# Three engines' orders changed inside the turn, and one joint stretch in place of the last three turns

## The chip, the cores and the metric

The kernel runs on one core of a Trainium2 chip. The metric is the device time of one execution in microseconds; lower is better. The core's engines run side by side, each through its own list of instructions, and wait for each other by semaphores: TensorE (PE, matmuls and transposes), VectorE (DVE), ScalarE (ACT), GpSimd (POOL) and SyncE (SP, which here issues the DMAs).

## What is computed

For 32 sequences of 512 tokens, three stages with residual sums. Cut to what matters:

```python
h = tok(x, mask)                 # running counts of each skill, mapped to 64 features
h = h + attn(layernorm(h))       # a decayed linear-attention recurrence over the batches' positions
h = h + ffn(layernorm(h))        # mixture of 8 experts, the best 2 weighted by softmax

def ffn(x):                      # xn = layernorm(x) * gamma + beta
    logits = xn @ Wr + br;  w = softmax of the top 2, scattered over 8 experts
    for e in range(8):
        h_e = gelu(xn @ W1[e] + b1[e]);  y += (h_e @ W2[e] + b2[e]) * w[:, e]

def attn(v):                     # per step: x_t = (0.97*x + relu(v @ Dx.T)) / sum
    a = rho @ x_t;  y = relu(ln(a) @ Dy.T) * relu(x_t);  out = ln(y @ E.T);  rho = 0.97*rho + outer(ln(v), x_t)
```

## The kernel before, in words

After a preamble (counts, features, factors) the kernel goes through the 32 batches in turns. A batch is 512 tokens (4 chunks of 128). Turn i does four things at once, each for another batch: the attention of batch i (`att`), the residual and the centring of batch r = i - 1 (`res`), the router of batch t = i - 2 (`rt`), and the experts of batch k = i - 3 (`mlp`). Batch i - 4 is finished (`done`), and the inputs of batch i + 1 are made ready (`ahead`). Turns 0 to 3 fill the pipe, turns 4 to 29 are a loop of two turns a round, turns 30 and 31 are written out, and turns 32, 33 and 34 empty the pipe without attention. Each engine has its own `turn` function: its order of calls is the order in which the engine works, and nothing overtakes.

One turn, by what hangs on what:

- TensorE: `scores(i, 0..3)` (L1331) from the scanned inputs `xs` into two PSUM banks; `input_rows` and `state_of` for the carried state (L1342, L1353); `values` (L1366, L1370); `y_core` (L1392); `attn_var`; `update(i + 1, 0)` and `update(i + 1, 1)` (L1320), the pre-activation of the next batch, each into the bank that a gate has read; `z_out` (L1412); `z_rows` (L1421). Between them stand the router's `centred_T` and `logits` (L1431, L1440), eight `hidden(k, e)` (two matmuls each, L1449 and L1450, into two banks in turn), four `expert_out(k, q)` (L1461), `weights_T` (L1469) and `fold` (L1485).
- VectorE: `diagonal(i, 0..3)`, the causal mask on a scores block (L985); `residual(r)` (L1016), which waits for GpSimd's z_scaling; the router in small steps (L1021 to L1063); `weigh(k, q)` (L1072), the expert output times its weights; `gate` (L1001); `scan_input` (L970) and two scans (L979) for the next turn; `finish` (L992).
- ScalarE: `gelu(k, e)` (L605), one for each hidden; copies of PSUM (`centred_T` L598, `weights_T` L616, `z_T` L621, `attn_T` L584); `centred_high(r)` (L593), the f16 high part of the centred input; `z_square` (L628) and `h_square` (L636).
- GpSimd: `z_scale` (L423, L426), `centred` (L431 to L437), `centred_input` (L410), `centred_low(r)` (L447), which waits for `centred_high`, then `mean_back(r)` (L442) and `weighted_input(i + 1)` (L417), then `add_pairs` (L453), which waits for the scans; `add_halves` and `add_experts` (L457, L463).
- SyncE: stores a batch's router weights to DRAM and reads them back broadcast over the partitions (`spread`, two DMAs of 512 KB), loads the scan's factors, stores the output.

Hidden 0..7 use two banks, so `hidden(k, e)` waits for `gelu(k, e - 2)`. `scores(i, 3)` waits for `diagonal(i, 1)`, since both use one bank. `scores(i, 0)` waits for both scans.

Of the kernel before, what the change touches and what calls it, by code (L numbers as in the profile page):

```python
# [24 lines left out]
P = 128  # L25
# [6 lines left out]
E = 8  # L32
# [44 lines left out]
def program(nc, x, r, skill_w, skill_b, att_w, att_b, mast_w, mast_b, proj_w, proj_b, Ea, Dx, Dy, gamma, beta,  # L77
            Wr, br, W1, b1, W2, b2, ident, masks, decays, out):
    with ExitStack() as ctx:
# [116 lines left out]
        last_acc, last_both = relu_b[:, 0, :], relu_b[:, 1, 0:S // 2]  # L196
# [3 lines left out]
        ld_w3 = sem("ld_w3")  # L200
        ld_rows = [sem(f"ld_rows{n}") for n in range(4)]
# [39 lines left out]
        dv_relu, dv_sum = sem("dv_relu"), sem("dv_sum")  # L241
# [24 lines left out]
        def of_half(rows, half):  # L266

            chunks = rows.rearrange("p (c n) -> p c n", c=C)
            return chunks[:, 0:C:C - 1] if half == 0 else chunks[:, 1:C - 1]

# [7 lines left out]
        def _(sp):  # L278
# [47 lines left out]
            def store(b):  # L326
                sp.wait_ge(dv_out, b + 1)
                sp.dma_start(out[bass.ds(b, 1)].rearrange("o (c p) d -> p (o c) d", p=P), o_sb[:]).then_inc(st_out, 16)

            def spread(b, side):  # L330
# [32 lines left out]
        def _(pool):  # L363
# [102 lines left out]
            def turn(i, att, res, rt, mlp, done, ahead, side):  # L466
# [15 lines left out]
                if mlp and (not isinstance(i, int) or i < B + 2):  # L482
# [16 lines left out]
            turn(B, False, True, True, True, True, False, 0)  # L499
            turn(B + 1, False, False, True, True, True, False, 1)  # L500
            turn(B + 2, False, False, False, True, True, False, 0)
# [3 lines left out]
        def _(act):  # L505
# [94 lines left out]
            def gelu(b, e):  # L600
# [4 lines left out]
                act.activation(hid[:, e, :], h_bank[e % 2][:, :], ACT.Gelu, bias=b1T[:, e:e + 1],  # L605
# [34 lines left out]
            def turn(i, att, res, rt, mlp, done, ahead, side):  # L640
                r, t, k = i - 1, i - 2, i - 3
                if rt and not (isinstance(i, int) and i > B):
                    centred_T(t, side)
# [25 lines left out]
                if res:  # L669
                    centred_high(r)  # L670
                if rt:
                    weights_T(t)
                if mlp:
                    gelu(k, 5)
                    gelu(k, 6)
# [16 lines left out]
            turn(B, False, True, True, True, True, False, 0)  # L692
            turn(B + 1, False, False, True, True, True, False, 1)
            turn(B + 2, False, False, False, True, True, False, 0)
# [3 lines left out]
        def _(dve):  # L698
# [377 lines left out]
            def last_sum(q):  # L1076

                dve.wait_ge(dv_tm, NP * (B - 1) + q + 1)
                wait(dve, dv_sum, q - 1)
                dve.tensor_tensor(last_acc, tm[:, 0, :] if q == 1 else last_acc, tm[:, q, :], ALU.add).then_inc(dv_sum, 1)  # L1080

            def last_halves():
                dve.wait_ge(dv_sum, NP - 1)
                dve.tensor_tensor(last_both, last_acc[:, 0:S // 2], last_acc[:, S // 2:S], ALU.add).then_inc(dv_sum, 1)

            def turn(i, att, res, rt, mlp, done, ahead, side):
# [28 lines left out]
                final = isinstance(i, int) and i == B + 2  # L1115
# [9 lines left out]
                if final:  # L1125
                    last_sum(1)
# [8 lines left out]
                if mlp:  # L1135
                    weigh(k, 2, 1 - side)
                    if final:
                        last_sum(2)
                    weigh(k, 3, 1 - side)
                if final:  # L1140
                    last_sum(3)
                    last_halves()
# [13 lines left out]
            turn(B, False, True, True, True, True, False, 0)  # L1156
            turn(B + 1, False, False, True, True, True, False, 1)
            turn(B + 2, False, False, False, True, True, False, 0)
            finish(B - 1)
# [3 lines left out]
        def _(pe):  # L1163
# [260 lines left out]
            def centred_T(b):  # L1424
# [4 lines left out]
                wait(pe, dv_out, b - 2)  # L1429
# [35 lines left out]
            def weights_T(b):  # L1465

                pe.wait_ge(dv_w, b + 1)
                wait(pe, dv_out, b - 2)
                pe.transpose(ly_w, w_flat[:], ident_f[:]).then_inc(pe_wT2, 1)  # L1469

            def fold(b):

                total = both
                if isinstance(b, int) and b == B - 1:
                    pe.wait_ge(dv_sum, NP)
                    total = last_both
                else:
                    pe.wait_ge(po_acc, b + 1)
                if isinstance(b, int):
                    pe.wait_ge(ac_wT, min(b + 3, B))  # L1480
                else:
                    pe.wait_ge(ac_wT, b + 3)
                for c in range(2):
                    y = ly[:, 256:512].rearrange("p (n c d) -> p c n d", n=2, c=2)[:, c]
                    last = pe.transpose(y, total[:, c * P:(c + 1) * P], ident_f[:])  # L1485
                last.then_inc(pe_fold, 1)

            def turn(i, att, res, rt, mlp, done, ahead, side):
                r, t, k = i - 1, i - 2, i - 3
                ending = isinstance(i, int) and i > B  # L1490
                if att:
                    scores(i, 0)
                if rt and not ending:
# [8 lines left out]
                if rt and not ending:  # L1502
# [8 lines left out]
                if mlp:  # L1511
                    hidden(k, 3, 1 - side)
                    if ending:
                        expert_out(k, 0)
                    if not att:
# [110 lines left out]
```

## Time and profile before

| | us |
|---|---|
| median of 3 runs | 698.47 (698.41 to 698.85) |
| profiled execution | 698.65 |
| its span, first to last instruction | 696.9 |
| busy: TensorE, VectorE, ScalarE, GpSimd | 636.0, 552.2, 436.6, 341.8 |
| mean granted TensorE clock | 0.99 of full speed |

Times in the profile are microseconds from the start of the span. A busy share says how full an engine is, not who waits for whom; a group of instructions has a line of the kernel, a count, a time and what released the engine before it. PE stands for matmuls and PEld for the weight loads ahead of them, which overlap matmuls.

### The profile page before, as it was taken

The page shows a single profiled execution, that of the slowest core. Times are in us where ns is not written, and L with a number is a line of the kernel's source. Part 1 is how long each engine was busy: PE and PEld are TensorE (multiplying, and loading weights), DVE is VectorE, ACT ScalarE, POOL GpSimd, SP SyncE. Part 2 cuts the span into 40 slices and gives each one's busy share as a digit, 9 for nine tenths or more (in the row PEclk, how much of TensorE's full clock was granted, in tenths as well). Part 3 has the DMA queues.
Part 4 walks back from the last instruction along what each step waited for, and adds up shares of the span by engine and source line. Part 5 has one row for each costly group of instructions (what it writes and reads, how often), then busy time and mean ns, then how long its engine had stood idle before and what let it go on. Part 6 is the DMA issues. An engine that isn't in the chain of part 4 may idle for free.

```text
span 696.9 us, 19160 instructions
## 1 busy us (share of the span) xinstructions
PE 636.0 (91%) x5027; PEld 428.5 (61%) x5064; DVE 552.2 (79%) x1956; ACT 436.6 (63%) x1385; POOL 341.8 (49%) x440
## 2 busy tenths in 40 slices
PE   1582997989999999999999999999999999999986
PEld 0472774456666666666666666666666666667542
DVE  4998888976688888888788888887888888887574
ACT  6980997024566666666666666666666666666663
POOL 2000001933465665566666665566656655666552
PEclk9999998899999999999999999999999999999999
DMA  6200000011434444444445444444444444454444
GB/s 214 98 0 1 1 0 1 25 40 35 94 92 102 99 99 99 112 111 109 111 110 117 117 101 99 99 99 99 99 99 99 99 99 114 106 111 100 94 80 84
DMA packets 61295, 60.41 MB, mean 87 GB/s; under 512 B 21796, under 2 KB 56724, under 8 KB 60756
## 3 DMA queue, kind: packets, MB, share of 16 engines
q1 hardware_dynamic: 58836, 59.34, 35.7%
q10 hardware_dynamic: 2240, 0.73, 0.5%
q8 instruction: 13, 0.21, 0.1%
q14 instruction: 14, 0.11, 0.0%
q0 software_dynamic: 192, 0.01, 0.0%
HBM read 55.18 MB, written 4.89 MB: 86 GB/s over the span
## 4 chain that ended last, share of the span: by engine, by line
PE 75%; DVE 10%; ACT 8%; issue 5%; ACTq 1%; DMA 1%; SPq 0%; DVEq 0%
PE bank L1461 16%; PE bank L1331 13%; PE bank L1449 7%; PE bank L1450 6%; PE bank L1392 5%; PE bank L1412 4%; PE bank L1353 4%; ACT skill_rows L605 3%; PE bank L1366 3%; PE bank L1237 2%; PE bank L1370 2%; PE bank L1342 2%; PE bank L1188 2%; PE bank L1226 2%; PE bank L1217 2%
## 5 line engine op out<-in xcount | busy, mean ns | idle before, releaser
L605 ACT ACTIVATE skill_rows<-bank,b1T,w_scale 128x512 f32<-128x512 f32 x256 | 195.1, 777 | 60.7 <-PE bank L1450 59.2
L1461 PE MATMUL bank<-skill_rows,w_sb 128*64 128x256 f32 x1024 | 128.6, 383 | 0.0
L453 POOL TENSOR_TENSOR feat_parts<-skill_rows 128x512 f32<-128x512 f32 x62 | 78.9, 1272 | 75.7 <-DVE feat_parts L979 67.8
L1331 PE MATMUL bank<-feat_parts 128*128 128x256 f32 (+1 forms) x512 | 104.4, 337 | 1.4 <-DVE feat_parts L979 0.9
L1461 PEld LDWEIGHTS bank<-skill_rows,w_sb 128*64 128x64 f32 x1024 | 69.1, 137 | 42.5 <-issue 12.9
L1331 PEld LDWEIGHTS bank<-feat_parts 128*128 128x128 f32 x512 | 77.3, 190 | 12.0 <-DVE feat_parts L985 6.5
L1001 DVE SCALAR_TENSOR_TENSOR feat_parts<-bank,feat_parts 128x256 f32<-128x256 f32 x128 | 45.4, 418 | 46.1 <-PE bank L1392 46.1
L979 DVE TENSOR_TENSOR_SCAN feat_parts<-same,feat_parts 128x512 f32<-128x512 f32 x62 | 74.3, 1238 | 0.0
L1072 DVE SCALAR_TENSOR_TENSOR skill_rows<-bank,b2T,feat_parts 128x256 f32<-128x256 f32 x128 | 54.2, 474 | 7.6 <-issue 4.8
L628 ACT ACTIVATE bank<-bank 128x64 f32<-128x64 f32 x128 | 26.7, 221 | 50.9 <-PE bank L1421 50.9
L1072 DVE SCALAR_TENSOR_TENSOR skill_rows<-bank,b2T,skill_rows 128x256 f32<-128x256 f32 x128 | 54.3, 473 | 4.2 <-PE bank L1461 2.9
L568 ACT ACTIVATE feat_parts<-bank 128x128 f32<-128x128 f32 x64 | 17.6, 275 | 61.6 <-DVE feat_parts L985 61.6
L1016 DVE SCALAR_TENSOR_TENSOR h_all<-bank,z_scaling,h_all 128x64 f32 (+1 forms) x128 | 27.5, 278 | 31.6 <-POOL z_scaling L426 31.6
L1449 PE MATMUL bank<-xT_even,w1k 128*128 128x512 f16 x128 | 48.8, 381 | 2.7 <-ACT skill_rows L605 1.8
L1449 PE MATMUL bank<-xT_odd,w1k 128*128 128x512 f16 x128 | 48.8, 381 | 2.3 <-ACT skill_rows L605 1.3
L1450 PE MATMUL bank<-xT_odd,w1k 128*128 128x512 f16 x128 | 48.5, 379 | 0.0
L1450 PE MATMUL bank<-xT_even,w1k 128*128 128x512 f16 x128 | 48.5, 379 | 0.0
L431 POOL TENSOR_TENSOR h_var<-h_sq,eps_sq 128x4 f32<-128x4 f32 x32 | 6.5, 203 | 80.9 <-ACT h_squares L636 80.9
L457 POOL TENSOR_TENSOR feat_parts<-feat_parts 128x512 f32<-128x512 f32 x31 | 39.3, 1269 | 2.4
L970 DVE SCALAR_TENSOR_TENSOR feat_parts<-bank,same 128x512 f32<-128x512 f32 x62 | 39.7, 681 | 0.0
L985 DVE TENSOR_TENSOR feat_parts<-bank,mask_sb 128x128 f32<-128x128 f32 x128 | 35.6, 278 | 4.0 <-PE bank L1331 3.8
L1392 PE MATMUL bank<-aT,dyT 64*128 64x256 f32 x256 | 36.3, 402 | 0.0
(266 smaller groups left out, 1446.1 us busy)
## 6 DMA issues: line engine op xcount, KB each, us to landing
skill_rows<-w_d SPq DMA_DIRECT2D x32, 512.0 KB, 6.5
feat_parts<-w_d SPq DMA_DIRECT2D x32, 512.0 KB, 6.3
same<-factor_d SPq DMA_DIRECT2D x31, 512.0 KB, 5.2
skill_rows<-skill_row_d SPq DMA_DIRECT2D x4, 1024.0 KB, 7.8
out<-o_sb SPq DMA_DIRECT2D x32, 128.0 KB, 4.9
w_sb<-in_L_ffn_W ACTq DMA_DIRECT2D x2, 256.0 KB
w_d<-wT SPq DMA_DIRECT2D x32, 16.0 KB, 1.4
table_k<-table_d SPq DMA_DIRECT2D x9, 2.5 KB
```

Of the source, the lines that this page charges most:

```text
L453: pool.tensor_tensor(half[:, n, :], tm[:, 2 * n, :], tm[:, 2 * n + 1, :], ALU.add).then_inc(po_half, 1)
L457: pool.tensor_tensor(acc.rearrange("p two t -> p (two t)"), half[:, 0, :], half[:, 1, :], ALU.add)\
L605: act.activation(hid[:, e, :], h_bank[e % 2][:, :], ACT.Gelu, bias=b1T[:, e:e + 1], scale=w1_scale[:, e:e + 1]).then_inc(ac_gelu, 1)
L970: dve.scalar_tensor_tensor(relu_b[:, k, :], n_bank[k][:, :], 0.0, factor[:, 1, :], ALU.max, ALU.mult)\
L979: dve.tensor_tensor_scan(xs[:, k, :], factor[:, 0, :], relu_b[:, k, :], 0.0, ALU.mult, ALU.add)\
L1001: dve.scalar_tensor_tensor(of_half(ys[:, k], half), core[:, k], 0.0, of_half(xs[:, k], half), ALU.max, ALU.mult).then_inc(dv_y, 1)
L1072: last = dve.scalar_tensor_tensor(tm[:, q, cols], z_bank[q % 2][:, cols], b2T[:, e:e + 1], wb[side][:, e, :], ALU.add, ALU.mult)
L1331: last = pe.matmul(n_bank[sc % 2][:, 0:SPAN[sc]], xs[:, k, sc * P:(sc + 1) * P], xs[:, k, sc * P:sc * P + SPAN[sc]], start=(k == 0), stop= ...
L1392: last = pe.matmul(n_bank[half][:, k * 2 * P:(k + 1) * 2 * P], dyT[rows, k * P:(k + 1) * P], aT[rows, :], start=True, stop=True)
L1449: pe.matmul(h_bank[e % 2][:, :], w1k[:, 0, e, :], xT[side][:], start=True, stop=False)
L1450: pe.matmul(h_bank[e % 2][:, :], w1k[:, 1, e, :], xT[side][:], start=False, stop=True).then_inc(pe_hid, 1)
L1461: last = pe.matmul(z_bank[q % 2][n * D:(n + 1) * D, at:at + S // 2], w2_sb[:, e, :], hid[:, e, n * (S // 2):(n + 1) * (S // 2)], start=Tru ...
```

## The change

Inside a turn, three orders change. VectorE does `diagonal(i, 1)` before `residual(r)`. ScalarE does `weights_T(t)` and `gelu(k, 5)` before `centred_high(r)`. TensorE does `hidden(k, 6)` between the two `update` calls.

Turn 31 now also holds `centred_T` and `logits` of batch 30, on TensorE and ScalarE. Turns 32 to 34 and the last fold go. In their place each engine gets a `drain()` for batches 29, 30 and 31 together. In it the hiddens use four banks, the expert outputs three banks by a written list, the two GpSimd sums of the last batch are replaced by transposes that accumulate in PSUM (`last_fold`), the last batch's weights are read back in four DMAs with two semaphores, and the last four stores have output tiles of their own. The matmuls that only kept TensorE busy there (`keep_running`) go.

```diff
@@ scalar turn
                 if mlp:
                     gelu(k, 4)
+                if rt:
+                    weights_T(t)
+                if mlp:
+                    gelu(k, 5)
                 if res:
                     centred_high(r)
-                if rt:
-                    weights_T(t)
-                if mlp:
-                    gelu(k, 5)
+                if mlp:
                     gelu(k, 6)
                     gelu(k, 7)
-                if isinstance(i, int) and i == B:
+                if isinstance(i, int) and i == B - 1:
                     centred_T(r, 1 - side)
@@ vector turn
                 if att:
                     diagonal(i, 0)
+                    diagonal(i, 1)
                 if res:
                     residual(r)
-                if att:
-                    diagonal(i, 1)
@@ tensor turn
                 if ahead:
                     update(i + 1, 0)
+                if mlp:
+                    hidden(k, 6, 1 - side)
+                if ahead:
                     update(i + 1, 1)
-                if mlp:
-                    hidden(k, 6, 1 - side)
...
+                if done:
+                    fold(i - 4)
+                if mlp:
                     hidden(k, 7, 1 - side)
-                if isinstance(i, int) and i == B:
+                if before_drain:
                     centred_T(r)
                 if att:
                     z_out(i)
...
@@ sync
+            def spread_last(side):
+                sp.wait_ge(ac_wT, B)
+                sp.dma_start(w_d[side].rearrange("e (c p) -> (e c) p", c=C), wT[:]).then_inc(st_w, 16)
+                sp.wait_ge(st_w, 16 * B)
+                for late, signal in enumerate((ld_wb, ld_wb_late)):
+                    experts = slice(late * NP, (late + 1) * NP)
+                    for n in range(2):
+                        rows = w_d[side:side + 1, experts, n * (S // 2):(n + 1) * (S // 2)]
+                        sp.dma_start(wb[side][n * D:(n + 1) * D, experts], rows.to_broadcast([D, NP, S // 2]))\
+                          .then_inc(signal, 16)
...
-            turn(B, False, True, True, False, 0)
-            turn(B + 1, False, True, True, False, 1)
-            turn(B + 2, False, False, True, False, 0)
-            store(B - 1)
+            spread(B - 2, 0)
+            spread_last(1)
+            for n in range(4):
+                store(B - 4 + n, last_o[n])
@@ gpsimd
+            def drain():
+                z_scale(B - 1)
+                add_pairs(B - 4, 1)
+                centred(B - 1)
+                centred_low(B - 1)
+                add_halves(B - 4)
+                add_experts(B - 4)
+                mean_back(B - 1)
+                for b in (B - 3, B - 2):
+                    add_pairs(b, 0)
+                    add_pairs(b, 1)
+                    add_halves(b)
+                    add_experts(b)
@@ scalar
+            def drain():
+                a, b, c = B - 3, B - 2, B - 1
+                for e in range(3):
+                    gelu(a, e, drain_h)
+                h_square(c)
+                tanh(b)
+                for e in range(3, 6):
+                    gelu(a, e, drain_h)
+                centred_high(c)
+                weights_T(b)
+                for e in range(6, E):
+                    gelu(a, e, drain_h)
+                centred_T(c, 1)
+                for e in range(4):
+                    gelu(b, e, drain_h)
+                tanh(c)
+                for e in range(4, 6):
+                    gelu(b, e, drain_h)
+                weights_T(c)
+                for e in range(6, E):
+                    gelu(b, e, drain_h)
+                for e in range(E):
+                    gelu(c, e, drain_h)
@@ vector
+            def drain():
+                a, b, c = B - 3, B - 2, B - 1
...
+                residual(c)
...
+                drain_weigh(a, 0)
+                drain_weigh(a, 1)
+                drain_weigh(a, 2)
...
+                merge(c, m)
+                drain_weigh(a, 3)
+                drain_finish(B - 4)
+                for q in range(NP):
+                    drain_weigh(b, q)
+                drain_finish(a)
+                for q in range(NP):
+                    drain_weigh(c, q)
+                drain_finish(b)
+                last_finish()
@@ tensor
+            def drain():
+                a, b, c = B - 3, B - 2, B - 1
+                for e in range(6):
+                    drain_hidden(a, e)
+                drain_out(a, 0)
+                drain_hidden(a, 6)
+                drain_out(a, 1)
+                weights_T(b)
+                drain_hidden(a, 7)
+                drain_out(a, 2)
+                drain_hidden(b, 0)
+                centred_T(c)
...
+                drain_out(a, 3)
+                logits(c, 1)
...
+                drain_out(b, 1)
+                weights_T(c)
...
+                drain_fold(B - 4)
+                for e in range(4):
+                    drain_hidden(c, e)
+                drain_out(b, 2)
+                drain_out(b, 3)
+                drain_hidden(c, 4)
+                drain_hidden(c, 5)
+                drain_out(c, 0)
+                drain_hidden(c, 6)
+                drain_hidden(c, 7)
+                drain_fold(a)
+                drain_out(c, 1)
+                for e in range(2):
+                    last_fold(0, e)
+                drain_out(c, 2)
+                for e in range(2):
+                    last_fold(1, e)
+                drain_out(c, 3)
+                drain_fold(b)
+                for q in range(2, NP):
+                    for e in range(2):
+                        last_fold(q, e)
```

`before_drain` is turn 31. In the VectorE stretch `residual(c)` stands inside the router of b, and `merge(c)` ends the whole router of c. `drain_weigh`, `drain_out` and `drain_hidden` do what `weigh`, `expert_out` and `hidden` do, with the banks and waits of the new stretch; `drain_weigh(c, 2)` and `drain_weigh(c, 3)` also wait for the later two of the four DMAs, and `drain_out(b, 3)` waits for `drain_weigh(b, 0)`, whose bank it takes.

## Rows read from the trace of the kernel before

**Rows 1.** Busy time of each engine over the whole execution, from the page.
```profile
PE 636.0 (91%) x5027; PEld 428.5 (61%) x5064; DVE 552.2 (79%) x1956; ACT 436.6 (63%) x1385; POOL 341.8 (49%) x440
```

**Rows 2.** Waits, 411.7 to 641.9: who for whom; us in total, times, longest.
```profile
PEld bank L1449 <- ACT skill_rows L605: 3.8, 13, 0.3
...
PEld bank L1331 <- DVE feat_parts L985: 2.6, 13, 0.2
```

**Rows 3.** Timeline of one turn: start, us, engine, line, operation [idle before <- releaser].
```profile
406.30 0.78 ACT L605 ACTIVATE skill_rows<-bank,b1T,w_scale 128x512 f32<-128x512 f32 x1 [1.80 <-PE bank L1450]
...
406.98 0.40 ACT L593 ACTIVATE x_p<-xc 128x256 f16<-128x256 f32 x1
...
407.28 0.25 ACT L616 ACTIVATE wT<-bank 32x128 f32<-32x128 f32 x1
...
407.44 2.23 ACT L605 ACTIVATE skill_rows<-bank,b1T,w_scale 128x512 f32<-128x512 f32 x3
407.46 0.68 POOL L447 TENSOR_TENSOR x_p<-xc,x_p 128x256 f16<-128x256 f32 x1 [0.97 <-ACT x_p L593]
...
408.25 0.39 PE L1449 MATMUL bank<-xT_odd,w1k 128*128 128x512 f16 x1
...
408.67 0.61 POOL L417 TENSOR_TENSOR same<-h_all,u_scale 128x256 f32 x1
...
409.06 2.41 DVE L979 TENSOR_TENSOR_SCAN feat_parts<-same,feat_parts 128x512 f32<-128x512 f32 x2
...
409.70 1.90 PE L1461 MATMUL bank<-skill_rows,w_sb 128*64 128x256 f32 x16
...
411.80 1.03 PE L1331 MATMUL bank<-feat_parts 128*128 128x256 f32 x4
...
412.67 0.39 PE L1431 MATMUL bank<-ident_h,x_p 128*128 128x128 f16 x4
...
414.21 0.38 PE L1449 MATMUL bank<-xT_even,w1k 128*128 128x512 f16 x1
...
414.74 1.61 PE L1331 MATMUL bank<-feat_parts 128*128 128x256 f32 x8
...
416.19 0.38 PE L1449 MATMUL bank<-xT_even,w1k 128*128 128x512 f16 x1
```

**Rows 4.** Timeline, turn 0 into turn 1: scans, then the scores that wait.
```profile
151.99 2.33 DVE L979 TENSOR_TENSOR_SCAN feat_parts<-same,feat_parts 128x512 f32<-128x512 f32 x2
...
154.37 1.13 PE L1331 MATMUL bank<-feat_parts 128*128 128x256 f32 x4 [0.32 <-DVE feat_parts L979]
```

**Rows 5.** The bias add: all 32 (least/median/most ns), one beside GpSimd's add.
```profile
L1026 DVE TENSOR_TENSOR lg<-lg,br_sb x32: 191/1198/1232, 171.3 to 672.8; 128x32 f32<-128x32 f32 x32
...
201.76 1.27 POOL L457 TENSOR_TENSOR feat_parts<-feat_parts 128x512 f32<-128x512 f32 x1
...
201.88 1.20 DVE L1026 TENSOR_TENSOR lg<-lg,br_sb 128x32 f32<-128x32 f32 x1
```

**Rows 6.** Timeline of the end, from turn 31's first scores on.
```profile
642.09 1.03 PE L1331 MATMUL bank<-feat_parts 128*128 128x256 f32 x4
...
658.20 0.44 PE L1421 MATMUL bank<-ident_f,zT_sb 128*128 128x128 f32 x2
...
661.09 0.86 DVE L1016 SCALAR_TENSOR_TENSOR h_all<-bank,z_scaling,h_all 128x64 f32<-128x64 f32 x4 [1.89 <-POOL z_scaling L426]
...
663.80 0.24 ACT L636 ACTIVATE h_squares<-h_all 128x64 f32<-128x64 f32 x1
...
667.08 0.42 ACT L593 ACTIVATE x_p<-xc 128x256 f16<-128x256 f32 x1 [1.57 <-POOL xc L437]
667.41 0.25 ACT L616 ACTIVATE wT<-bank 32x128 f32<-32x128 f32 x1
...
677.16 1.66 DVE L1072 SCALAR_TENSOR_TENSOR skill_rows<-bank,b2T,skill_rows 128x256 f32<-128x256 f32 x4 [0.23 <-DMA skill_rows<-w_d]
...
694.04 0.42 DVE L992 TENSOR_TENSOR o_sb<-bank,h_all 128x256 f32<-128x256 f32 x1 [0.53 <-PE bank L1485]
```

More of the change, by code:

```diff
@@ L195, in program @@
         both = sb("both", [P, S // 2])
-        last_acc, last_both = relu_b[:, 0, :], relu_b[:, 1, 0:S // 2]
+        last_tm = over(parts_flat, 2 * S, NP, S)
+        last_o = [over(parts_flat, n * C * D, C, D) for n in range(4)]
         o_sb = sb("o_sb", [P, C, D])
@@ L604, in gelu @@
                 wait(act, pe_zz, NP * (b - 1) + e // 2 + 1)
[L605 removed]
+                act.activation(hid[:, e, :], banks[e % len(banks)][:, :], ACT.Gelu, bias=b1T[:, e:e + 1],
                                scale=w1_scale[:, e:e + 1]).then_inc(ac_gelu, 1)
@@ L1074, in weigh, with drain_weigh @@
                 last.then_inc(dv_tm, 1)
[L1076 to L1084, printed above, removed]
+            def drain_weigh(b, q):
+                dve.wait_ge(pe_zz, NP * b + q + 1)
+                dve.wait_ge(ld_wb, 32 * (b + 1))
+                z = drain_z[b - (B - 3)][q]
+                if b == B - 1 and q >= NP // 2:
+                    dve.wait_ge(ld_wb_late, 32)
+                if b < B - 1:
+                    wait(dve, po_half, 2 * (b - 1) + q // 2 + 1)
+                for n in range(2):
+                    e, cols = 2 * q + n, slice(n * (S // 2), (n + 1) * (S // 2))
+                    last = dve.scalar_tensor_tensor((tm if b < B - 1 else last_tm)[:, q, cols], z[:, cols],
+                                                    b2T[:, e:e + 1], wb[b % 2][:, e, :], ALU.add, ALU.mult)
+                    if b == B - 1:
+                        last.then_inc(dv_last, 1)
+                if b < B - 1:
+                    last.then_inc(dv_tm, 1)
@@ L1155, in _ @@
             turn(B - 1, True, True, True, True, True, False, 1)
[L1156 to L1159, printed above, removed]
+            drain()
         @block.tensor
@@ L1428, in centred_T @@
                 wait(pe, ac_wT, b)
-                wait(pe, dv_out, b - 2)
+                wait(pe, dv_out, b - 2 if not isinstance(b, int) else min(b - 2, B - 4))
                 for c in range(C):
@@ new lines, in drain_out @@
+            def drain_out(b, q):
+                pe.wait_ge(ac_gelu, E * b + 2 * q + 2)
+                if b == B - 3 or (b == B - 2 and q == 0):
+                    pe.wait_ge(dv_tm, NP * b + q - 1)
+                elif b == B - 2 and q == 1:
+                    pe.wait_ge(dv_h, C * B)
+                elif b == B - 1 and q == 3:
+                    pe.wait_ge(dv_last, 2)
+                else:
+                    pe.wait_ge(dv_tm, NP * b + q - 2)
+                z = drain_z[b - (B - 3)][q]
+                for e in range(2 * q, 2 * q + 2):
+                    at = (e - 2 * q) * (S // 2)
+                    for n in range(2):
+                        last = pe.matmul(z[n * D:(n + 1) * D, at:at + S // 2], w2_sb[:, e, :],
+                                         hid[:, e, n * (S // 2):(n + 1) * (S // 2)], start=True, stop=True)
+                last.then_inc(pe_zz, 1)
@@ new lines, in drain_fold, with last_fold @@
+            def drain_fold(b):
+                wait(pe, dv_out, b)
+                fold(b, 4)
+            def last_fold(q, e):
+                if q + e == 0:
+                    pe.wait_ge(ac_gelu, E * B - 2)
+                pe.wait_ge(dv_last, 2 * q + e + 1)
+                for c in range(2):
+                    at = e * (S // 2) + c * P
+                    last = pe.matmul(h_bank[c][:, 0:P], last_tm[:, q, at:at + P], ident_f[:], start=(q + e == 0),
+                                     stop=(2 * q + e == E - 1))
+                if 2 * q + e == E - 1:
+                    last.then_inc(pe_fold, 1)
@@ L1501, in turn @@
                     hidden(k, 1, 1 - side)
-                if rt and not ending:
+                if rt:
                     logits(t, side)
@@ L1550, in turn @@
                     expert_parts_T()
-                if ending:
+                if done:
+                    fold(i - 4)
+                if mlp:
                     hidden(k, 7, 1 - side)
-                if done:
-                    if isinstance(i, int) and i == B:
-                        keep_running(4, n_bank[0])
-                    fold(i - 4)
-                if mlp and not ending:
-                    hidden(k, 7, 1 - side)
-                if isinstance(i, int) and i == B:
+                if before_drain:
                     centred_T(r)
```

127 lines of the change are left out of this document (72 added, 55 removed).

## The prediction

> **What bounds the kernel now.** I read the engine totals first: TensorE is busy 91% of the span and no other engine above 79% [rows 1]. The loop is a turn per batch; the first scores group of a turn starts at 411.80 us and fourteen turns later at 642.09 [rows 3, 6], so a turn is 16.45 us. Twenty-eight turns (3 to 30) have both an expert stage and a scan for the next turn. The waits of fourteen turns show what stands in TensorE's way [rows 2]: 0.29 us a turn before `hidden(k, 7)`, on a gelu, and 0.20 before a scores group, on a mask product of VectorE. The timeline of one turn then shows two paths that both close at the next `scores(i, 0)`. TensorE's own: gelu 4, centred_high (L593), weights_T (L616), gelu 5, `hidden(k, 7)` at 408.25, then z_out, four expert outputs' worth of matmuls, z_rows, scores at 411.80. VectorE's: y_core, gates, one weigh, scan inputs, the two scans, which end at 409.06 + 2.41 = 411.47 [rows 3]. In a turn where TensorE waited for the scans, scores began 0.05 after their end (154.32 to 154.37) and took 1.13 instead of 1.03 [rows 4]. So the scans would let scores go at 411.52, with 0.10 for the slower start: VectorE's path has only 411.80 - 411.62 = 0.18 us of slack. Who shortens TensorE alone gains 0.18 a turn.
>
> **The turn, part by part.** *Mask product 1 before the residual.* It now needs only `scores(i, 1)` and fits into the time VectorE waits for z_scaling. The last two scores groups take 416.19 - 414.74 = 1.45; a 256-wide group takes 412.67 - 411.80 = 0.87, so one and a half of those 1.31 [rows 3]. The gain is 0.14 (bounds 0 and the 0.20 of the wait). It lies ahead of y_core and so shortens both paths. The residual starts about 0.1 later; nothing that it feeds is late.
>
> *weights_T and gelu 5 before centred_high.* centred_high's place is 407.28 - 406.98 = 0.30 long, so gelu 5 starts 0.30 earlier and the wait of 0.29 before `hidden(k, 7)` goes [rows 2, 3]. I take 0.2 for TensorE's path (bounds 0.1 and 0.29), because fold and the moved pre-activation lie right ahead of it. What moves back is centred_high: behind weights_T (407.44 - 407.28 = 0.16) and gelu 5 (0.68, the step from gelu 4 to what follows), 0.84 later. GpSimd's centred_low (L447), mean_back (L442) and weighted_input (L417) stand in its queue behind centred_high, so they begin at 408.30 instead of 407.46, the third at 409.51 instead of 408.67, and it ends at 410.12 instead of 409.28 [rows 3]. Their products are wanted in the next turn, which has room. The scan is not indifferent to them.
>
> *update 1 behind hidden 6.* update 1 waited for the second gate, hidden 6 for gelu 4; gelu 4 ends at 407.08, as the gates do. TensorE stands until about 407.1 either way, and the second scan input is not due before the first has run: nothing, bounds 0.1 either way.
>
> *What the shifted GpSimd work costs.* VectorE's bias add (two operands in SBUF, 32 columns) began at 201.88, 0.12 into a GpSimd add of 1.27, and ended with it after 1.20; the least of its 32 durations is 0.19 [rows 5]. The scan too reads two SBUF operands. Its pair takes 2.33 with GpSimd quiet and 2.41 where L417 ran 0.22 into it [rows 3, 4]. So a scan waits for the GpSimd instruction under way. The Trainium skill, "SBUF — State Buffer", section "Who interferes with whom", says the same: such an instruction and a GpSimd instruction that reads SBUF shut each other out for a whole instruction, whoever issues first. It doesn't say who goes next when both queues are full, and that is what the sum hangs on; it gives no number here.
>
> In the new order the scan comes at 409.06 upon L442, which ends at 409.51; before, what it met ended at 409.28. The first scan is 0.23 later at least. Then three outcomes: (a) VectorE gets both scans through before L417: 0.23. (b) L417 gets in between the scans: 0.23 and between 0.45 and 0.61 more, I take 0.45, so 0.68. (c) L417 goes ahead of both: 0.84. No row shows two full queues. Against (c): the scan has been waiting when L442 ends, and L417 only begins then. The second scan is issued 0.09 before the first ends, which speaks for (a); that L417 would have waited longest speaks for (b). I take (a), without much conviction.
>
> VectorE's path: -0.18 slack, -0.14 mask, +0.23: -0.09 a turn. TensorE's path: -0.14 - 0.2 = -0.34, no longer the limit. Over 28 turns: -2.5 us.
>
> **The last three batches.** Before, the last z_rows is at 658.20, the last finish begins at 694.04, and 696.9 - 694.46 = 2.4 remain for the store [rows 6]. The new stretch gives gelu four banks, folds the last batch by accumulation on TensorE, and splits the last weights' load. In steps:
> 1. Turn 31 now holds centred_T(30) ahead of z_out. It needs L447, which ends at 408.14 + 0.84 = 408.98 in turn time, while `hidden(k, 7)` is done 0.43 after 408.05 (0.43: from 414.21 to 414.74, less some 0.1 of the logits between [rows 3]). TensorE stands 0.5; with its transposes of 0.2 and the gain of 0.2 the last z_rows is 0.5 later, 658.7.
> 2. residual(31) ends 661.95 - 658.20 = 3.75 later: 662.45. The squares follow at once at 662.5, not behind the tanh at 663.80. From there to centred_high was 3.28 and to weights_T 0.33 more [rows 6]: 666.1 for batch 30's weights instead of 667.41.
> 3. From weights_T to the weigh that waited for its broadcast was 677.16 - 667.41 = 9.75: 675.85.
> 4. Batch 31's weights_T waits for all four weighs of batch 29, the last of which VectorE has behind batch 31's whole router. I put it between 673.0 and 674.6, from when gelu 3 of batch 30 lets the tanh go and whether the bias add is shut out once; taken late, 674.6 and 9.75: 684.4 for all experts, the first half sooner.
> 5. TensorE meanwhile: out(30, 3) needs weigh(30, 0), 676.7; behind it in its queue stand four hiddens of 0.43 and four pairs of 0.93 (409.70 row, halved [rows 3]), folds, and the waits between them, as the weighs of 31 (0.83 each by the row of four, [rows 6]) alternate with the outputs. That puts the last weigh's end at 687.4, the accumulated folds and the finish at 688.4, the end at 690.8. With batch 31's weights at 673.0 it is 689.2.
>
> A gain of 6.1 to 7.7; I take 6.5. If the four broadcasts share so badly that the landing is 3 us later, 3 is left; if the weights' waits fall away, 9. ScalarE needs 24 gelus of 0.68, 16.3 us, of some 28: it hides.
>
> **Sum.** Against the profiled execution (698.65; span 696.9, 1.75 around it; the median of the runs is 698.47, 0.2 less): 698.65 - 2.5 - 6.5 = 689.65, say 689.6. A change under 0.2% (1.4 us) can hardly be told from none.
>
> **Rivals.**
> - *L417 between the scans* (b): +0.68 - 0.32 = +0.36 a turn, +10.1; with the end's -6.5, 702.2. For it: GpSimd has waited longest. Against: the scans follow each other without a gap. It turns the sign once the scans end 0.32 + 6.5/28 = 0.55 later than now. This is the slower side.
> - *L417 before both* (c): +0.52 a turn, +14.6: 706.7.
> - *The port doesn't bite*: GpSimd's shifted work finds another place or the scan slips in ahead of L442. Both paths give -0.32: -9.0 - 6.5, 683.1. Against it: [rows 3, 4] show the scan already being held.
> - *The stretch at the end doesn't gain*: waits for broadcasts and banks eat it (gain 2 or less), with (a): 694 to 696.
>
> **How the numbers follow.** (a) 0.42, (b) 0.31, (c) 0.07, no port effect 0.13, end without gain 0.07. The likeliest gives 689.6; its own range is 687 to 693 by the end's bounds of 3 and 9. To hold 8 in 10 the range must reach (b) with its own 1.3 above and below, since (a) and (b) are 12.6 apart: 684.5 to 703.5, which leaves out (c) and most of the no-port case. Faster by over 0.2%: (a), no port, most of the end case: 0.59. Within: the edges of (b) and of the end case: 0.08. Slower: 0.33.
>
> **What the profile will show.** L447 about 0.8 later against the gates; the wait before `hidden(k, 7)` gone; scores 2 and 3 in 1.31. The scan pair: 2.6 under (a), 3.1 with the second scan long under (b), both turns' length following; L417 long under (a), since it is shut out. A wait on VectorE's scan before scores. In the end: z_rows(31) 0.5 later in its turn, about 25 us from the weights of batch 30 to the end. I am wrong if the turn's length moves by more than 0.15 while the scan pair stays at 2.4 to 2.65, or if the last stretch waits for the final broadcasts beyond 685.

## The result, and the profile after

The changed kernel takes 703.9 us (median of 4 runs, 703.08 to 705.05) against 698.66: a ratio of 1.0076, 95% interval 1.0058 to 1.0093. It is slower; the forecast said 689.6 and at most 703.5. The profiled execution took 703.08, its span is 701.3 (before 696.9).

A full turn in the middle, all engines' timeline, where [rows 3] stood for before. The lines of the kernel moved: L634 is gelu, L645 weights_T, L622 centred_high, L1549 a hidden, L463 centred_low, L458 mean_back, L433 weighted_input, L1032 the scans, L1431 the scores. The instruction at 410.89 is gelu 5, the one at 411.76 `hidden(k, 7)`:

```profile
410.05 0.78 ACT L634 ACTIVATE skill_rows<-bank,b1T,w_scale 128x512 f32<-128x512 f32 x1 [1.79 <-PE bank L1550]
...
410.73 0.25 ACT L645 ACTIVATE wT<-bank 32x128 f32<-32x128 f32 x1
...
410.89 0.76 ACT L634 ACTIVATE skill_rows<-bank,b1T,w_scale 128x512 f32<-128x512 f32 x1
...
411.55 0.40 ACT L622 ACTIVATE x_p<-xc 128x256 f16<-128x256 f32 x1
...
411.76 0.38 PE L1549 MATMUL bank<-xT_odd,w1k 128*128 128x512 f16 x1
...
412.03 0.67 POOL L463 TENSOR_TENSOR x_p<-xc,x_p 128x256 f16<-128x256 f32 x1 [1.91 <-ACT x_p L622]
...
412.66 0.61 POOL L458 TENSOR_TENSOR h_all<-h_all,mean_h  x1
412.81 3.03 DVE L1032 TENSOR_TENSOR_SCAN feat_parts<-same,feat_parts 128x512 f32<-128x512 f32 x2
...
413.23 1.53 POOL L433 TENSOR_TENSOR same<-h_all,u_scale 128x256 f32 x1
...
415.89 1.13 PE L1431 MATMUL bank<-feat_parts 128*128 128x256 f32 x4 [0.43 <-DVE feat_parts L1032]
```

The wait before `hidden(k, 7)` (411.76) is gone: gelu 5 starts 0.84 after gelu 4, before it was 1.14. But the pair of scans takes 3.03 instead of 2.41, and weighted_input 1.53 instead of 0.61. Read the ends: mean_back ends at 413.27, weighted_input at 414.76, the scans at 415.84. And TensorE, which reached the scores without a wait before, now stands 0.43 for the scans. This is the same in the fourteen turns of the view of waits from 411.7 to 641.9 (us in total, times, longest), in place of [rows 2]:

```profile
PEld bank L1431 <- DVE feat_parts L1032: 9.3, 14, 0.7
...
PE bank L1431 <- DVE feat_parts L1032: 6.0, 14, 0.4
```

Neither of the two rows of [rows 2] is left. The durations of the 62 single scans in the turns say it in one row (least, median, most, ns):

```profile
L1032 DVE TENSOR_TENSOR_SCAN feat_parts<-same,feat_parts x62: 1195/1544/1568, 151.4 to 649.7; 128x512 f32<-128x512 f32 x62
```

Turn 31's scores, and the end, where [rows 6] stood. L1521 is z_rows, L1140 a weigh of the end stretch, L1152 the last finish:

```profile
651.36 1.13 PE L1431 MATMUL bank<-feat_parts 128*128 128x256 f32 x4 [0.35 <-DVE feat_parts L1032]
...
668.04 0.44 PE L1521 MATMUL bank<-ident_f,zT_sb 128*128 128x128 f32 x2
...
675.49 0.25 ACT L645 ACTIVATE wT<-bank 32x128 f32<-32x128 f32 x1
...
683.37 0.27 ACT L645 ACTIVATE wT<-bank 32x128 f32<-32x128 f32 x1 [0.58 <-DVE skill_rows L1140]
...
684.73 1.66 DVE L1140 SCALAR_TENSOR_TENSOR skill_rows<-bank,b2T,skill_rows 128x256 f32<-128x256 f32 x4
...
696.26 0.88 DVE L1140 SCALAR_TENSOR_TENSOR feat_parts<-bank,b2T,feat_parts 128x256 f32<-128x256 f32 x2 [1.22 <-PE bank L1608]
...
698.41 0.49 DVE L1152 TENSOR_TENSOR feat_parts<-bank,h_all 128x128 f32<-128x128 f32 x2 [0.94 <-PE bank L1624]
```

The account of the 4.4 us, from the two traces. A turn lasts (651.36 - 415.89) / 14 = 16.82 instead of 16.45, so the turns bring 0.37 each. Turn 31's scores come 651.36 - 642.09 = 9.27 later: less than 28 x 0.37 = 10.4, since turn 3's scores are at 180.30 instead of 181.25. Of this 0.95, 0.31 is the mask order's: from turn 1's scores to turn 3's it takes 26.6 in every trace that has this order, and 26.9 in every one without it (26.56 and 26.87 in these two). The rest lies ahead of turn 1's scores and is no effect that these runs can show: over all traces of this document turn 3's scores stand anywhere between 180.28 and 182.66, and x2 and y1, with the same code up to there, have 182.13 and 180.28. Turn 31 up to z_rows takes 16.68 instead of 16.11: +0.57. From z_rows to the end it is 33.3 instead of 38.7: -5.4. Together 9.27 + 0.57 - 5.4 = +4.4.

### The profile page after: what moved, and what is told of

Read it like the earlier page. It is cut to its first block, busy times and chain, and to the rows that moved or that the text cites. A ratio compares the mean times of both kernels' runs of the same rounds, so it can differ in the third digit from the quotient of the medians.

```text
span 701.3 us, 19220 instructions
## 1 busy us (share of the span) xinstructions
PE 638.0 (91%) x5077; PEld 432.0 (62%) x5077; DVE 552.8 (79%) x1953; ACT 442.6 (63%) x1385; POOL 365.8 (52%) x440
## 4 chain that ended last, share of the span: by engine, by line
PE 56%; DVE 24%; issue 13%; ACT 3%; DVEq 2%; DMA 1%; POOL 1%; SPq 0%; ACTq 0%; POOLq 0%
PE bank L1431 13%; DVE feat_parts L1032 8%; PE bank L1561 8%; PE bank L1492 5%; DVE feat_parts L1054 4%; PE bank L1453 4%; PE bank L1549 3%; PE bank L1550 3%; PE bank L1466 3%; DVE skill_rows L1125 2%; PE bank L1442 2%; PE bank L1470 2%; PE bank L1288 2%; PE bank L1326 2%; PE bank L1337 2%
## 5 line engine op out<-in xcount | busy, mean ns | idle before, releaser
L634 ACT ACTIVATE skill_rows<-bank,b1T,w_scale 128x512 f32<-128x512 f32 x256 | 192.9, 770 | 67.2 <-PE bank L1550 65.6
L1431 PE MATMUL bank<-feat_parts 128*128 128x256 f32 (+1 forms) x512 | 105.2, 338 | 13.7 <-DVE feat_parts L1032 12.7
L1561 PE MATMUL bank<-skill_rows,w_sb 128*64 128x256 f32 x928 | 116.4, 382 | 0.0
L1431 PEld LDWEIGHTS bank<-feat_parts 128*128 128x128 f32 x512 | 79.4, 190 | 26.7 <-DVE feat_parts L1032 20.1
L1032 DVE TENSOR_TENSOR_SCAN feat_parts<-same,feat_parts 128x512 f32<-128x512 f32 x62 | 91.6, 1516 | 0.0
L1561 PEld LDWEIGHTS bank<-skill_rows,w_sb 128*64 128x64 f32 x928 | 63.1, 137 | 37.4 <-issue 11.4
L1125 DVE SCALAR_TENSOR_TENSOR skill_rows<-bank,b2T,skill_rows 128x256 f32<-128x256 f32 x120 | 50.8, 473 | 4.0 <-PE bank L1561 2.8
L463 POOL TENSOR_TENSOR x_p<-xc,x_p 128x256 f16<-128x256 f32 x32 | 21.5, 672 | 56.8 <-ACT x_p L622 56.8
L1125 DVE SCALAR_TENSOR_TENSOR skill_rows<-bank,b2T,feat_parts 128x256 f32<-128x256 f32 x112 | 47.4, 472 | 1.3
L433 POOL TENSOR_TENSOR same<-h_all,u_scale 128x256 f32 (+1 forms) x32 | 45.3, 1416 | 4.2 <-PE bank L1470 4.1
L1549 PE MATMUL bank<-xT_even,w1k 128*128 128x512 f16 x120 | 45.7, 381 | 0.1
L1550 PE MATMUL bank<-xT_even,w1k 128*128 128x512 f16 x120 | 45.5, 379 | 0.0
L1549 PE MATMUL bank<-xT_odd,w1k 128*128 128x512 f16 x112 | 42.7, 381 | 0.0
L1550 PE MATMUL bank<-xT_odd,w1k 128*128 128x512 f16 x112 | 42.4, 379 | 0.0
```

Of the source, the lines that this page charges most:

```text
L433: pool.tensor_tensor(ub[:], h_of(b), wide(u_scale[:, bass.ds(b * C, C)], D), ALU.mult).then_inc(po_ub, 1)
L634: act.activation(hid[:, e, :], banks[e % len(banks)][:, :], ACT.Gelu, bias=b1T[:, e:e + 1], scale=w1_scale[:, e:e + 1]).then_inc(ac_gelu, 1)
L1032: dve.tensor_tensor_scan(xs[:, k, :], factor[:, 0, :], relu_b[:, k, :], 0.0, ALU.mult, ALU.add)\
L1125: last = dve.scalar_tensor_tensor(tm[:, q, cols], z_bank[q % 2][:, cols], b2T[:, e:e + 1], wb[side][:, e, :], ALU.add, ALU.mult)
L1431: last = pe.matmul(n_bank[sc % 2][:, 0:SPAN[sc]], xs[:, k, sc * P:(sc + 1) * P], xs[:, k, sc * P:sc * P + SPAN[sc]], start=(k == 0), stop= ...
L1549: pe.matmul(h_bank[e % 2][:, :], w1k[:, 0, e, :], xT[side][:], start=True, stop=False)
```

## Experiments

Theory P: the scans lose time to GpSimd instructions that hold an SBUF port, since centred_high's move pushes them under the scans. Rivals: U, the later second pre-activation holds the scan inputs back; E, the end stretch costs; Q, GpSimd's chain is late, and the port has no part in it.

The turn length is the distance of the first scores row near 410 or 427 from that of turn 31, divided by the turns between. The scan pair runs from the first scan's start to the second one's end. Each ratio is to executions of the kernel before that were timed with that run (medians 698.49 to 699.0), and can differ by 0.0015 from the quotient of the medians; 698.66 is their median beside the changed kernel. Line numbers differ a little from kernel to kernel:

| kernel | what differs | scan pair | turn | median | ratio to before (95%) |
|---|---|---|---|---|---|
| before | | 2.41 | 16.45 | 698.66 | |
| after | all of the change | 3.03 | 16.82 | 703.9 | 1.0076 (1.0058 to 1.0093) |
| x2 | after, GpSimd's two early | 2.33 | 16.13 | 686.05 | 0.983 (0.9809 to 0.9852) |
| x4 | after, one of the two early | 2.67 | 16.45 | 693.54 | 0.9935 (0.9916 to 0.9954) |
| x1 | after, ScalarE's order back | 2.42 | 16.39 | 691.68 | 0.9898 (0.9882 to 0.9915) |
| x3 | after, all three orders back | 2.41 | 16.44 | 693.71 | 0.9927 (0.991 to 0.9943) |
| k1 | x2 and two adds that read SBUF | 3.09 | 16.89 | 706.66 | 1.0118 (1.0101 to 1.0135) |
| k2 | x2 and two memsets | 2.33 | 16.13 | 685.13 | 0.9813 (0.9796 to 0.9829) |
| s1 | before, ScalarE's order new | 3.02 | 16.98 | 713.48 | 1.0208 (1.0191 to 1.0226) |
| s2 | before, mask order new | 2.41 | 16.38 | 696.72 | 0.9969 (0.9958 to 0.998) |
| s3 | before, pre-activation order new | 2.41 | 16.45 | 698.3 | 0.9994 (0.9985 to 1.0003) |
| y1 | x2, last outputs first | 2.33 | 16.13 | 684.26 | 0.9802 (0.9785 to 0.9818) |
| z1 | y1, pre-activation order back | 2.33 | 16.15 | 685.99 | 0.9814 (0.9801 to 0.9828) |
| z2 | y1, mask order back | 2.33 | 16.29 | 689.41 | 0.9868 (0.9853 to 0.9883) |

**x2: GpSimd's two instructions ahead of centred_low.** In GpSimd's turn:

```diff
                 if ahead:
                     centred_input(i + 1)
                 if res:
-                    centred_low(i - 1)
                     mean_back(i - 1)
                 if ahead:
                     weighted_input(i + 1)
+                if res:
+                    centred_low(i - 1)
```

> The changed kernel, but in the turn GpSimd does mean_back and weighted_input before centred_low, so that only centred_low stands behind the later centred_high. Theory P (the loss is GpSimd's instructions that hold the SBUF port when the scans come): the scan pair goes from 3.03 us to about 2.35, centred_low ends just ahead of it, the turn shortens from 16.82 to 16.13 (16.45 before, less 0.18 slack and 0.14 of the mask product), and the time is 703.9 - 28 x 0.69 = 684.6. Rival U (the second pre-activation now comes a hidden later and holds back the second scan input and all behind it): nothing moves, 703.9. Rival E (the end stretch is what costs): nothing moves, 703.9.

Turn 16.13 and 686.05. The timeline of x2:

```profile
419.11 0.61 POOL L458 TENSOR_TENSOR h_all<-h_all,mean_h  x1
...
419.68 0.61 POOL L433 TENSOR_TENSOR same<-h_all,u_scale 128x256 f32 x1
...
421.06 0.67 POOL L463 TENSOR_TENSOR x_p<-xc,x_p 128x256 f16<-128x256 f32 x1 [0.77 <-ACT x_p L623]
...
421.85 2.33 DVE L1033 TENSOR_TENSOR_SCAN feat_parts<-same,feat_parts 128x512 f32<-128x512 f32 x2
...
424.34 1.03 PE L1432 MATMUL bank<-feat_parts 128*128 128x256 f32 x4
```

GpSimd is done at 421.73, the scan starts at 421.85 and the pair has its clear 2.33; the scores no longer wait. One call moved behind two others gives back all that the turn had lost and 0.32 a turn more. U and E would have left 703.9. That the turn is exactly the 16.13 of the expectation is partly luck: its sum took VectorE's path for the limit, but here the scores start 0.16 after the scans' end (424.18) without a wait for them, so TensorE's path sets the turn. For that path the forecast had 16.45 - 0.34 = 16.11.

**x4: one of the two.**

```diff
                     centred_input(i + 1)
+                    weighted_input(i + 1)
                 if res:
                     centred_low(i - 1)
                     mean_back(i - 1)
-                if ahead:
-                    weighted_input(i + 1)
```

> The changed kernel, but only weighted_input is moved ahead of centred_low; mean_back stays behind it and still reaches into the first scan. Theory P: the first scan waits for the rest of mean_back, 0.2 to 0.25 us, and nothing gets in between the scans, pair about 2.6, turn 16.36, time 703.9 - 28 x 0.46 = 691.0. This is the case that the forecast took to be the likeliest. Rivals U and E: 703.9.

```profile
408.00 0.62 POOL L458 TENSOR_TENSOR h_all<-h_all,mean_h  x1
408.15 2.67 DVE L1031 TENSOR_TENSOR_SCAN feat_parts<-same,feat_parts 128x512 f32<-128x512 f32 x2
...
410.87 1.13 PE L1430 MATMUL bank<-feat_parts 128*128 128x256 f32 x4
```

The pair is 2.67, so the rest of mean_back costs 0.26 over the 2.41 of before, as the forecast's case (a) had it. The turn is 16.45, not 16.36: the mask order brought less than thought (below). So even case (a) would have left the turn where it was, and the time at 693.5.

**x1: ScalarE's order back.**

```diff
                     gelu(k, 4)
+                if res:
+                    centred_high(r)
                 if rt:
                     weights_T(t)
                 if mlp:
                     gelu(k, 5)
-                if res:
-                    centred_high(r)
-                if mlp:
                     gelu(k, 6)
```

> The changed kernel with ScalarE's order in the turn as before (centred_high before weights_T and gelu 5). Theory P: scan pair back to 2.41, the wait before hidden 7 back at 0.29 us a turn, the mask product's 0.14 stays: turn 16.31, 703.9 - 28 x 0.51 = 689.6, and up to 0.5 less since turn 31 no longer waits for centred_low. Rival U: the loss stays, 703.9 or a little more. Rival E: 703.9.

The pair is 2.42, the wait before hidden 7 is back (4.1 us in 13 times in its view of waits), the turn is 16.39: 0.08 more than expected, and 691.68 by the same.

**x3: the end alone.** x1's edit, and the other two orders of the turn as before:

```diff
                     diagonal(i, 0)
-                    diagonal(i, 1)
                 if res:
                     residual(r)
+                if att:
+                    diagonal(i, 1)
...
                     update(i + 1, 0)
+                    update(i + 1, 1)
                 if mlp:
                     hidden(k, 6, 1 - side)
-                if ahead:
-                    update(i + 1, 1)
```

> All three orders in the turn as before, with turn 31's router work and the new end stretch kept. Theory P and rival U: turn 16.45, and the end stretch alone, read from the two traces as 4.9 us shorter: 698.66 - 4.9 = 693.8, perhaps 0.5 less since turn 31 has its centred_high earlier. Rival E (the end costs, the turn is neutral): 703 or more.

693.71, turn 16.44: the end stretch by itself is a gain of 0.7%, and E falls. Its trace shows where the end stretch can lose time. L337 issues the store of batch 30's weights to DRAM, L341 the two broadcasts that read them back:

```profile
665.30 0.25 ACT L645 ACTIVATE wT<-bank 32x128 f32<-32x128 f32 x1
...
665.57 0.32 SPq L337 DMA_DIRECT2D w_d<-wT  x1
...
669.27 1.26 SPq L341 DMA_DIRECT2D skill_rows<-w_d  x2
...
677.03 1.27 DVE L1139 SCALAR_TENSOR_TENSOR skill_rows<-bank,b2T,skill_rows 128x256 f32<-128x256 f32 x3 [2.57 <-DMA skill_rows<-w_d]
```

From the weights' copy to the first weigh that needs their broadcast it took 11.73 here, and 9.24 in the changed kernel. The broadcasts are not what differs: from its issue to its landing the later of the two took 7.05 here and 6.86 there. The store of 16 KB ahead of them does: it took 3.68 here and 1.39 there, and the broadcasts are issued only when it has landed (3.70 and 1.41 after the store's issue). From z_rows (657.85) to the end (692.6) this trace needs 34.8; the traces of the changed kernel, x1, x2, x4, k1 and k2, with the same end stretch and a store of 1.4, need 33.2 or 33.3. `drain_out(b, 3)` waits for that weigh, and the last batch's hiddens stand behind it in TensorE's queue: the end hangs on a landing. Why the store took 2.3 longer stays open; z1 and z2 below have it too, and the edits don't touch it.

**k1 and k2: the port by itself.** x2, with two useless instructions behind `centred_low` in turns 3 to 30: k1 has the `tensor_tensor` line of this diff, k2 the `memset` line in its place. Their results are used by nobody; the output is complete.

```diff
+                if mlp and ahead:
+                    wait(pool, spare_done, 2 * (i - 3))
                 if res:
                     centred_low(i - 1)
+                if mlp and ahead:
+                    for n in range(2):
+                        pool.tensor_tensor(spare[:, n, :], mask_sb[:], mask_sb[:], ALU.add).then_inc(spare_done, 1)
+                        pool.memset(spare[:, n, :], 0.0).then_inc(spare_done, 1)
```

> The kernel with GpSimd's two instructions moved early (x2, 686.05 us), plus two useless GpSimd adds of 256 columns that read SBUF, right behind centred_low in turns 3 to 30. Nothing waits for them but GpSimd itself. Theory P: they hold the port at the scans as mean_back and weighted_input did: the scan pair goes from 2.33 to about 3.0 to 3.3, the turn from 16.13 to 16.85 to 17.1, the time to 706 to 713. Rival Q (what counted was that GpSimd's chain to the next turn's inputs was late, not the port): pair 2.33, time 686.

> The same place, but the two extra GpSimd instructions are memsets of 360 columns, which write SBUF and read nothing. If the port is shut by any GpSimd instruction: pair well over 2.4, time up to 713. If only by one that reads: pair 2.33, 686.

k1's timeline, then k2's:

```profile
413.15 0.68 POOL L465 TENSOR_TENSOR x_p<-xc,x_p 128x256 f16<-128x256 f32 x1 [0.84 <-ACT x_p L633]
...
413.78 2.10 POOL L469 TENSOR_TENSOR spare<-mask_sb 128x256 f32<-128x256 f32 x2
...
413.87 3.09 DVE L1043 TENSOR_TENSOR_SCAN feat_parts<-same,feat_parts 128x512 f32<-128x512 f32 x2
...
417.01 1.13 PE L1442 MATMUL bank<-feat_parts 128*128 128x256 f32 x4 [0.49 <-DVE feat_parts L1043]
```

```profile
420.17 0.67 POOL L465 TENSOR_TENSOR x_p<-xc,x_p 128x256 f16<-128x256 f32 x1 [0.84 <-ACT x_p L633]
...
420.78 0.74 POOL L469 MEMSET spare<- 128x360 f32 x2
...
420.89 2.33 DVE L1043 TENSOR_TENSOR_SCAN feat_parts<-same,feat_parts 128x512 f32<-128x512 f32 x2
```

Adds that nobody waits for bring the whole loss: turn 16.89, 706.66. Memsets at the same place, 0.63 us of them beside the first scan, bring none. Q falls, and the contention is one over reads. The two adds of k1 show the order of service in one row of that line, for all 56 of them (least, median, most, ns):

```profile
L469 POOL TENSOR_TENSOR spare<-mask_sb x56: 611/1071/1531, 194.2 to 650.8; 128x256 f32<-128x256 f32 x56
```

The median lies halfway between the least and the most, as it does where half of the adds take 0.61 and half 1.53; in the turn shown the first add runs 413.78 to 414.39 and the second ends at 415.88. So the second add was held for 0.92 by the first scan, then ran, and then the second scan ran.

**s1: ScalarE's order alone on the kernel before**, which is x1's diff the other way round.

> The kernel before with ScalarE's new order alone. Theory P: scan pair 3.03, no mask gain: turn 16.45 + 0.44 = 16.89, 698.5 + 12.3 = 711. Rival U (the late second pre-activation costs): no loss here, 698.5 or a few us less, since the wait before hidden 7 goes.

Turn 16.98 and 713.48, the worst of all: the one move costs 2.1%. Its pair is as in the changed kernel; without the mask order the front of the turn adds 0.16, more than the 0.07 that x1 had shown for it.

**s2, s3: the other two orders alone**, the first (s2) and the second part (s3) of x3's diff the other way round, on the kernel before.

> The kernel before with VectorE's mask product 1 ahead of the residual, nothing else. The forecast's step: 0.14 a turn, turn 16.31, 698.5 - 3.9 = 694.6. From x1, where turn 16.39 was seen with mask and pre-activation order together: 0.07 a turn, 696.5. Rival: the later residual eats it, 698.5.

> The kernel before with TensorE's hidden 6 between the two pre-activations, nothing else. The forecast's step: nothing, 698.5 within 0.2%. Rival U (the second scan input is held back): 0.1 us a turn or more, 701.3 or more.

The mask order gives 0.07 a turn and 0.3% (the interval excludes 1). The pre-activation order gives nothing that can be measured. U falls: both runs have the pair at 2.41.

**y1: the last outputs ahead of the accumulating transposes**, in TensorE's end stretch:

```diff
                 drain_out(c, 1)
-                for e in range(2):
-                    last_fold(0, e)
                 drain_out(c, 2)
-                for e in range(2):
-                    last_fold(1, e)
                 drain_out(c, 3)
                 drain_fold(b)
-                for q in range(2, NP):
+                for q in range(NP):
                     for e in range(2):
                         last_fold(q, e)
```

> x2 with one change in the end stretch: TensorE does the last batch's expert outputs 2 and 3 ahead of all accumulating transposes, not between them. In x2 VectorE stands 1.16 and 1.22 us before the last two weighs and 0.94 before the last finish. If TensorE's queue order makes those waits, 1.5 to 2.2 us go: 684. If the weights' landing makes them: 686.

```profile
671.64 2.81 PE L1609 MATMUL bank<-skill_rows,w_sb 128*64 128x256 f32 x24
...
674.66 3.74 PE L1625 MATMUL bank<-ident_f,feat_parts 128*128 128x128 f32 x32
...
678.44 0.49 DVE L1153 TENSOR_TENSOR feat_parts<-bank,h_all 128x128 f32<-128x128 f32 x2 [2.73 <-PE bank L1625]
```

The waits before the last weighs went, and came back as a wait of 2.73 for 32 transposes in a row, which take 3.7 us. From z_rows to the end the traces give 32.5 instead of 33.2, both with a store of 1.4; z1 and z2 below, which have this edit and a long store, give 34.0 and 34.2 where x3 gave 34.8. So by the traces the edit is worth 0.5 to 0.8, half or less of what was expected. The medians differ by 1.8, with intervals that overlap a little. The trace of y1 is 1.8 ahead of x2's at z_rows already, and all of that at turn 3's scores (180.28 and 182.13), which the edit doesn't touch. So 0.5 to 0.8 is shown, not 1.8. It is the fastest version, 2.0% under the kernel before.

**z1, z2: the two small orders in the fast turn:** y1 with the second (z1) or the first part (z2) of x3's diff.

> The fastest kernel so far (y1, 684.3) with the pre-activation order as before. Its turn is TensorE's alone. If that order is worth nothing here either: 684.3. If it fills TensorE's wait for the second gate, as it should where each 0.1 counts: up to 0.15 a turn lost, 688.5.

> The fastest kernel so far (y1, 684.3) with mask product 1 behind the residual as before. The mask order's worth in a turn that TensorE alone sets: 0.14 by the forecast's step, 688.2; 0.07 as in x1, 686.3.

The mask order is worth 16.286 - 16.133 = 0.15 a turn there, 4.3 us of the 5.2 measured. For the pre-activation order the trace gives 0.02 a turn, 0.6 us; the medians differ by 1.7, but the intervals overlap. The rest of z1's trace is lost before turn 1's scores (1.2 us, and x2's and y1's traces, with the same code there, differ by 1.8) and in the end stretch (34.0 instead of 32.5), where its store of batch 30's weights took 3.7 instead of 1.4. z2's end has such a store too (3.5). So 0.6 is what the trace shows of the pre-activation order, and the medians can't confirm it.

## Why the prediction was wrong

- **The step that failed**: "(a) VectorE gets both scans through before L417: 0.23", taken against "(b) L417 gets in between the scans [...] so 0.68". The trace shows (b): the first scan ends 1.08 after mean_back, weighted_input goes next, and the second scan ends 1.08 after that. The pair grew by 0.62, the turn by 0.37, where (b) had 0.68 and 0.36. That 0.36 is so close is luck: the first scan lost 0.24 (0.23 in the sum), but the second only 0.37, below the bounds of 0.45 and 0.61 set for it, and the mask order gave 0.07 instead of 0.14. The rival's time, 702.2, is 1.7 from the measured 703.9, outside its own bound of 1.3 by 0.4; the end stretch, 1.6 short of its 6.5, is most of that. The rest of the argument for the collision held: where GpSimd's instructions would stand, what they would meet, 0.84 later.
- **What would have been read right**: the rows gave the delay for one instruction and nothing for two full queues. The forecast said so and then gave the sign of the result to a preference of 0.42 to 0.31. The argument for (b), that the longest waiting is served next, was written down, and fits the changed kernel and k1. Whether the rule is that, or that the two engines take turns, no run here tells apart: each time the one that went next had also waited longest.
- **The mask order** was mis-sized for the turn of before: 0.14 forecast, 0.07 measured in s2, since the last two scores groups take 1.39 without the wait (418.94 to 420.33) and not one and a half times 0.87. In x2's turn and in s1's it is worth 0.15 and 0.16; there the wait without it is longer (4.0 us in 14 times, 0.3 at most, in z2's view of waits). With the right 0.07, (a) would have given no change of the turn, as x4 shows.
- **The slack** of VectorE's path, 0.18: x4's pair is 0.26 longer and its turn unchanged, so slack and mask order make 0.26, less the 0.07 of the mask: 0.19. The changed kernel gives the same: 0.62 - 0.37 = 0.25, less 0.07. Right.
- **gelu 5 and hidden 7**: the wait went; 0.2 was taken, and x2 against x1, 16.39 - 16.13, gives 0.26 (bounds 0.1 and 0.29). This is with the new mask order; without it z2 against the kernel before gives 16.45 - 16.29 = 0.16, so the two gains don't simply add. Right in kind, and worth nothing in the changed kernel, where TensorE's path isn't the limit.
- **update 1 behind hidden 6**: nothing, right.
- **The end**: 6.5 forecast, 4.9 measured (-5.4 and +0.57). Step 1, z_rows 0.5 late: 0.57. Steps 2 and 3: batch 30's weights 7.4 after z_rows by the forecast, 675.49 - 668.04 = 7.45; from the copy to the weigh 9.75, measured 9.24 in the changed kernel and 11.73 in x3, by the length of the store. Step 4: batch 31's weights 15.9 after z_rows, measured 15.33. Step 5 is where it fell short: the last weigh ends 29.1 after z_rows (28.7 forecast), but from there to the end of the finish it is 698.90 - 697.14 = 1.76 and not 1.0, as half of the 32 transposes are left, 1.95 us of them. And 6.5 was taken above the 6.1 that the steps themselves gave with the later weights.
- **Not in the forecast**: the mask order also took 0.31 out of turns 1 and 2.

## What to carry to other kernels

Before an instruction is moved on one engine, follow what stands behind it in the queues that it releases, and lay that beside the other engine's instructions with two SBUF operands: here an instruction whose result TensorE reads only 4.5 us after centred_low is done (408.14 and 412.67 in [rows 3]) pushed two GpSimd instructions under the scans that close the loop. When a VectorE and a GpSimd queue are both full of such instructions, don't count on the engine on the critical path to keep its place: here they alternated, and the GpSimd instruction between the scans, 0.61 long, cost the pair 0.37, after the 0.24 that the one already under way had cost. The cure costs nothing where the order is free: put the work that waits for nobody ahead of the wait (x2, 17.9 us of the changed kernel's 703.9).

## What the runs showed of the hardware

- VectorE and GpSimd, each with instructions ready that read two SBUF operands, took turns instruction by instruction: weighted_input, 0.61 alone, took 1.53, and the two scans 1.54 and 1.57 instead of 1.20 each. The wait is inside the recorded duration, so a held instruction looks busy, not idle. That two scans follow each other without a gap did not keep GpSimd out.
- GpSimd memsets of 0.40 us each beside the first scan left the pair at 2.33: writes alone didn't shut it out. The Trainium skill, "SBUF — State Buffer", section "Who interferes with whom", says the same (a GpSimd instruction that only writes doesn't contend); k1 and k2 agree with it, 3.09 against 2.33.
- The store of batch 30's weights, 16 KB from SBUF to DRAM, took 1.37 to 1.39 us in seven of the ten traces with the new end stretch and 3.5 to 3.7 in the other three (x3, z1, z2). The later of the two broadcasts of 512 KB behind it took 6.9 to 7.7 in all ten. So the first use of the weights moved by the store, 9.24 after their copy in the changed kernel and 11.73 in x3.
